# The first layer's score chunks in one group per pair: the next pair's first chunk is made a round ahead, in other banks

## What is computed

```python
q = einsum('qdh,bcd->bhcq', Q, x) * sq      # 16 heads of 64
k = einsum('qdh,bcd->bhcq', K, x) * sq
v = einsum('vdh,bcd->bhcv', V, x) * sv
att = where(causal, einsum('bhcq,bhCq->bhcC', q, k) / d_query, -inf)
y = einsum('bhcC,bhCv->bhcv', softmax(att), v)
z = einsum('dvh,bhcv->bcd', W, y) * scale   # back to 128 columns
```

## Time and profile before

| | |
|---|---|
| time, median of 3 runs | 1213.09 us (1210.03 to 1213.88) |
| profiled execution, first to last instruction | 1209.2 us |
| TensorE busy (matmul) | 1189.8 us, 98%, 8908 matmuls |
| TensorE loading weights (beside the matmuls) | 887.1 us, 73% |
| VectorE busy | 990.7 us, 82% |
| ScalarE busy | 819.7 us, 68% |
| GpSimd busy | 409.9 us, 34% |
| chain that ended last | TensorE 82%, VectorE 10%, ScalarE 4%, rest 4% |
| granted TensorE clock | full in all 40 slices |

### The profile page before, as it was taken

One profiled execution on the slowest core, in us unless ns is written; L12 is line 12 of the kernel. 1 busy time (PEld: TensorE's weight loads), 2 busy tenths in 40 slices (PEclk: granted clock), 3 DMA queues, 4 the chain that ended last, 5 costly groups with the idle time before them and its releaser, 6 DMA issues.

```text
span 1209.2 us, 23949 instructions
## 1 busy us (share of the span) xinstructions
PE 1189.8 (98%) x8908; PEld 887.1 (73%) x8908; DVE 990.7 (82%) x1918; ACT 819.7 (68%) x2174; POOL 409.9 (34%) x364
## 2 busy tenths in 40 slices
PE   8999999999999999999999999999999999999998
PEld 6777677767776777677767776777677767767766
DVE  6888588968886889688968896888788878988886
ACT  6785577567756775677567756775677768767875
POOL 2216420640064006400640064006400658535820
PEclk9999999999999999999999999999999999999999
DMA  7004300410041004200420042004200420000000
GB/s 258 1 30 134 97 1 21 132 61 2 20 134 62 1 19 134 62 1 19 135 62 1 20 134 62 1 17 136 62 1 16 138 62 2 7 12 19 1 11 27
DMA packets 44292, 63.93 MB, mean 53 GB/s; under 512 B 8144, under 2 KB 18384, under 8 KB 43920
## 3 DMA queue, kind: packets, MB, share of 16 engines
q1 hardware_dynamic: 44176, 62.39, 16.6%
HBM read 59.48 MB, written 2.88 MB: 52 GB/s over the span
## 4 chain that ended last, share of the span: by engine, by line
PE 82%; DVE 10%; ACT 4%; issue 2%; DMA 1%; SPq 1%; POOL 0%; DVEq 0%; ACTq 0%; POOLq 0%
PE psum L1435 14%; PE psum L1483 14%; PE psum L1505 12%; PE psum L64 9%; PE psum L66 9%; PE psum L65 9%; PE psum L1542 5%; DVE mneg L1123 2%; ACT probs L754 2%; PE psum L1444 2%; PE psum L1718 1%; DVE sg L1173 1%; PE psum L1509 1%; PE psum L1781 1%; DVE sg L1163 1%
## 5 line engine op out<-in xcount | busy, mean ns | idle before, releaser
L754 ACT ACTIVATE probs<-psum,mneg 128x512 f32<-128x512 f32 (+3 forms) x640 | 329.7, 529 | 127.1 <-DVE mneg L1123 122.5
L1123 DVE TENSOR_REDUCE mneg<-psum 128x2 f32<-128x1024 f32 (+2 forms) x320 | 253.6, 820 | 99.9 <-PE psum L1444 99.5
L1114 DVE COPY pt<-psum 128x512 f32<-128x512 f32 x320 | 205.2, 682 | 29.7 <-PE psum L1483 27.9
L1483 PE MATMUL psum<-ident,probs 128*128 128x128 f32 x1600 | 223.3, 278 | 6.1 <-DVE pt L1114 2.1
L1483 PEld LDWEIGHTS psum<-ident,probs 128*128 128x128 f32 x1600 | 176.5, 140 | 37.9 <-issue 19.5
L561 POOL TENSOR_TENSOR qk_lo<-sg,qk_hi 128x512 fp32r<-128x512 f32 x64 | 92.7, 1455 | 162.0 <-ACT qk_hi L798 162.0
L525 POOL TENSOR_TENSOR rstd<-var,mhalf 128x4 f32<-128x4 f32 x7 | 7.1, 1012 | 399.8 <-DVE var L1009 399.8
L1505 PE MATMUL psum<-pt,v_all 128*64 128x384 f32 (+5 forms) x1088 | 142.6, 412 | 0.0
L754 ACT ACTIVATION_READ_ACCUMULATOR probs<-psum,mneg 128x1 f32 x640 | 131.8, 206 | 0.0
L1435 PE MATMUL psum<-qk_hi 64*128 64x512 f32 (+7 forms) x640 | 121.6, 375 | 2.2 <-ACT probs L754 1.9
L1505 PEld LDWEIGHTS psum<-pt,v_all 128*64 128x64 f32 (+1 forms) x1088 | 69.5, 135 | 66.2 <-issue 50.7
(11 more groups left out here) (275 smaller groups left out, 2422.4 us busy)
## 6 DMA issues: line engine op xcount, KB each, us to landing
crow<-weights SPq DMA_DIRECT2D x256, 128.0 KB, 3.0
rrow<-sums SPq DMA_DIRECT2D x128, 128.0 KB, 3.0
gu_raw<-in_gu SPq DMA_DIRECT2D x1, 2176.0 KB, 11.5
x_all<-in_x SPq DMA_DIRECT2D x8, 256.0 KB, 6.4
out_rows<-x_all SPq DMA_DIRECT2D x7, 256.0 KB, 2.3
down_raw<-in_down SPq DMA_DIRECT2D x1, 1088.0 KB, 13.7
wqkv_raw<-in_wqkv SPq DMA_DIRECT2D x1, 896.0 KB, 6.8
wqkv_raw<-in_wqkv SPq DMA_DIRECT2D x1, 512.0 KB, 5.0
```

Of the source, the lines that this page charges most:

```text
L754: last = act.activation(probs[:, h * HALF + PROB[t]:h * HALF + PROB[t] + w], bank[score_bank(rnd, c) + h][:, o:o + w], ACT.Exp, bias=mneg[ ...
L1114: dve.tensor_copy(turned_rows(rnd)[:, s % 2, :, 3 - s // 2, :], turn_bank(rnd, s).rearrange("p (j q) -> p j q", q=P)).then_inc(pt_ready, 1)
L1123: last = dve.tensor_reduce(mneg_h[:, :, t], psum[:, b:b + 2, o:o + P * (t + 1)], AX, ALU.max, negate=True)
L1483: last = nc.tensor.transpose(turn_bank(rnd, s)[:, i * P:(i + 1) * P], probs[:, v:v + P], ident[:, :])
```

## The change

- The three chunks of a round become one group on TensorE (score_group): chunks 1 and 2 of pair n and chunk 0 of pair n+1. Each chunk's masks follow its own products. Chunk 0 uses banks 0 and 1, chunk 1 banks 2 and 3, chunk 2 banks 4 and 5.
- A round on TensorE is now: group; weighing of pair n-1; T0 and T1 of pair n; q and k of pair n+2; T4, T3 and T2 of pair n. Turns go to banks 7, 2, 6, 5, 4 for T0 to T4 (in round 0 to 6, 2, 7, 5, 4). Round 6 has the turn of the routing weights in place of q and k, round 7 that of the preceding batch's rows, both in bank 3; round 7's group has two chunks, and T4, T3 and T2 of its pair stand in units as before.
- q waits for the copy of y of pair n-1 (in round 0 for that of the accumulator), k for the copy of T0, chunk 1 for the copy of T1 (in round 7 for the copied routing weights too), chunk 2 for the copies of T4 and T3 and for the rests of pair n+1.
- ScalarE: exps of chunk 1, of chunk 2, copy_y(n-1), head 0 of the next pair's chunk 0 (next_exps), round_q(n+2), head 1 of that chunk, round_k(n+2), take_tile1(n).
- VectorE: maxima of chunks 1, 2 and the next pair's 0, routing step, copies of T0 and T1, inversion of sums, rest_q(n+2), copy of T3, rest_k(n+2), copy of T2.
- In units(b) T0, T1 and their waits are gone from the start, project_unit(b, 1) comes after a wait for the copy of T1 and for x1_ready in place of the waits for exponentials. The second layer keeps its banks and orders.

```diff
-SCORE_BANK = [0, 2, 0]
+SCORE_BANK = [0, 2, 4]
+SCORE_BANK1 = [0, 2, 0]
...
+        TURN_BANK0 = [7, 2, 6, 5, 4]
+        TURN_BANK0_FIRST = [6, 2, 7, 5, 4]
+
         def turn_bank(n, s):
+            if n < ROUNDS0:
+                return bank[(TURN_BANK0 if n % PAIRS else TURN_BANK0_FIRST)[s]]
...
-            return bank[6] if b < B - 1 else bank[7]
+            return bank[3] if b < B - 1 else bank[7]
+
+        WEIGHTS_BANK = bank[3]
...
-            if n < ROUNDS0 and n % PAIRS < 2:
-                return (bank[4], bank[5]) if n % PAIRS == 0 else (bank[6], bank[5])
+            if n < ROUNDS0 and n % PAIRS < 3:
+                return [(bank[4], bank[5]), (bank[6], bank[5]), (bank[7], bank[6])][n % PAIRS]
             return bank[6], bank[7]
...
+            def next_exps(rnd, h):
+
+                act.wait_ge(max_ready, max_count(rnd, 0))
+                act.wait_ge(turned, turn_count(rnd - 1, h))
...
                     if p == 0:
                         exps(n, 0)
+                        round_q(n + 1, SCALE0)
+                        round_k(n + 1)
+                    exps(n, 1)
+                    exps(n, 2)
+                    if p:
+                        copy_y(n - 1)
+                    elif b:
+                        copy_acc(b - 1)
                     if p < PAIRS - 1:
-                        round_q(n + 1, SCALE0)
-                    if p:
-                        take_tile1(n - 1)
-                        exps(n, 0)
+                        next_exps(n + 1, 0)
+                    if p < PAIRS - 2:
+                        round_q(n + 2, SCALE0)
                     if p < PAIRS - 1:
-                        round_k(n + 1)
-                    else:
+                        next_exps(n + 1, 1)
+                    if p < PAIRS - 2:
+                        round_k(n + 2)
+                    if p == PAIRS - 2:
                         copy_combt(b)
...
+                    take_tile1(n)
...
                     if p == 0:
                         row_maxima(n, 0)
-                        row_maxima(n, 1)
                         rest_q(n + 1, SCALE0)
                         rest_k(n + 1)
...
+                    row_maxima(n, 1)
+                    row_maxima(n, 2)
+                    if p < PAIRS - 1:
+                        row_maxima(n + 1, 0)
                     route(b, p)
+                    take_turned(n, [0, 1])
+                    invert_sums(n)
+                    if p < PAIRS - 2:
+                        rest_q(n + 2, SCALE0)
+                    if p < PAIRS - 1:
+                        take_turned(n, [3])
+                    elif b:
+                        add_rows(b - 1)
+                    if p < PAIRS - 2:
+                        rest_k(n + 2)
+                    if p < PAIRS - 1:
+                        take_turned(n, [2])
...
+            def turn_step0(n, s):
+
+                p = n % PAIRS
+                pe.wait_ge(exp_done, exp_count(n, [0, 1, 2, 2, 2][s]))
+                if s == 2:
+                    if p == 0:
+                        pe.wait_ge(qk_lo_ready, (n + 2) * 2 + 1)
+                    elif p < PAIRS - 2:
+                        pe.wait_ge(qk_lo_ready, (n + 2) * 2 + 1)
+                    else:
+                        pe.wait_ge(y_ready, n)
+                turn_blocks(n, s)
+
+            def score_group(n):
+
+                b, p = n // PAIRS, n % PAIRS
+                if p:
+                    pe.wait_ge(pt_ready, (n - 1) * (TURNS - 1) + 2)
+                if p == PAIRS - 1:
+                    pe.wait_ge(combt_ready, b + 1)
+                score0(n, 1)
+                if p:
+                    pe.wait_ge(pt4_ready, n)
+                    pe.wait_ge(pt_ready, (n - 1) * (TURNS - 1) + 3)
+                if p < PAIRS - 1:
+                    pe.wait_ge(qk_lo_ready, (n + 1) * 2 + 2)
+                score0(n, 2)
+                if p < PAIRS - 1:
+                    pe.wait_ge(exp_done, exp_count(n, 0))
+                    score0(n + 1, 0)
+
+            def slot(n):
...
                 if p == 0:
+                    first_head(b)
+                score_group(n)
+                if p:
+                    weigh_pair(n - 1)
+                elif b:
+                    project_out(b - 1, 3).then_inc(acc_done, 1)
+                turn_step0(n, 0)
+                turn_step0(n, 1)
+                if p < PAIRS - 2:
+                    if p:
+                        pe.wait_ge(y_ready, n)
+                    else:
+                        pe.wait_ge(acc_copied, b) if b else pe.wait_ge(logits_taken, 1)
+                    project_qk(n + 2, [0])
+                    pe.wait_ge(pt_ready, n * (TURNS - 1) + 1)
+                    project_qk(n + 2, [1])
+                elif p == PAIRS - 2:
+                    turn_weights(b)
+                elif b:
+                    turn_acc(b - 1)
                 if p < PAIRS - 1:
...
+                    turn_step0(n, 4)
+                    turn_step0(n, 3)
+                    turn_step0(n, 2)
...
             def first_head(b):
 
+                n = b * PAIRS
...
-                first_chunks(b)
-                score0(b * PAIRS, 1)
+                pe.wait_ge(qk_lo_ready, n * 2 + 2)
+                if b:
+                    pe.wait_ge(su_done, b * UNITS)
+                score0(n, 0)
+                pe.wait_ge(v_taken, (b + 1) * FILLS)
+                project_qk(n + 1, range(2))
                 if b:
                     project_out(b - 1, 2)
-                pe.wait_ge(v_taken, (b + 1) * FILLS)
-                project_qk(b * PAIRS + 1, range(2))
-                pe.wait_ge(exp_done, exp_count(b * PAIRS, 0))
-                score0(b * PAIRS, 2)
-                if b:
-                    project_out(b - 1, 3).then_inc(acc_done, 1)
```

More of the change, by code:

```diff
@@ L376, in max_count @@
         def max_count(n, c):
+            if n < ROUNDS0:
+                return n * NCH + c + 1
             return n * NCH + ([1, 2, 3] if first_round(n) else [1, 3, 2])[c]
         def score_bank(n, c):
-            return [6, 0, 6][c] if n >= ROUNDS0 and first_round(n) else SCORE_BANK[c]
+            if n < ROUNDS0:
+                return SCORE_BANK[c]
+            return [6, 0, 6][c] if first_round(n) else SCORE_BANK1[c]
         exp_count = max_count
@@ L756, in exps @@
                 last.then_inc(exp_done, 1)
+            def next_exps(rnd, h):
+                act.wait_ge(max_ready, max_count(rnd, 0))
+                act.wait_ge(turned, turn_count(rnd - 1, h))
+                t = CHUNKS[0][0]
+                o, s = h * HALF + PROB[t], slice(h * TILES + t, h * TILES + t + 1)
+                last = act.activation(probs[:, o:o + T], bank[score_bank(rnd, 0) + h], ACT.Exp, bias=mneg[:, s], accum_out=rsum[:, rnd % 2, s])
+                if h:
+                    last.then_inc(exp_done, 1)
             def take_values(b, fills):
@@ L811, in copy_combt @@
                 act.wait_ge(combt_done, b + 1)
-                act.activation(combt, bank[7][:, 0:P], ACT.Copy).then_inc(combt_ready, 1)
+                act.activation(combt, WEIGHTS_BANK[:, 0:P], ACT.Copy).then_inc(combt_ready, 1)
             def first_layer(b):
@@ L1523, in project_unit @@
                     pe.wait_ge(su_done, n - 1)
-                else:
-                    pe.wait_ge(exp_done, exp_count((b + 1) * PAIRS - 1, 2 - u))
                 half_unit(b, u, 0)
@@ L1585, in turn_weights @@
                 pe.wait_ge(comb_ready, b + 1)
-                nc.tensor.transpose(bank[7][:, 0:P], rexp[:, :, :].rearrange("p t e -> p (t e)"), ident[:, :]).then_inc(combt_done, 1)
+                nc.tensor.transpose(WEIGHTS_BANK[:, 0:P], rexp[:, :, :].rearrange("p t e -> p (t e)"), ident[:, :]).then_inc(combt_done, 1)
             def score0(n, c):
                 score_chunk(n, c, n % 2, ROWS0)
-            def first_chunks(b):
-                n = b * PAIRS
-                pe.wait_ge(qk_lo_ready, n * 2 + 2)
-                if b:
-                    pe.wait_ge(su_done, b * UNITS)
-                score0(n, 0)
-            def slot(n, head):
+            def turn_step0(n, s):
[26 more added lines that the diff above has]
+            def slot(n):
                 p = n % PAIRS
```

71 lines of the change are left out of this document (9 added, 62 removed).

## The result

| | before | after |
|---|---|---|
| median of 4 runs each | 1212.49 us (1210.03 to 1213.88) | 1233.1 us (1230.07 to 1233.91) |
| ratio, 95% interval | | 1.0165 (1.0146 to 1.0183) |
| profiled execution, first to last instruction | 1209.2 us | 1228.2 us |
| TensorE / VectorE / ScalarE busy | 1189.8 / 990.7 / 819.7 us | 1196.0 / 984.5 / 807.2 us |
| weighing to weighing, rounds 2 to 5 of a batch | 8.76 us | 9.05 to 9.08 us |

A forecast was written before the change was run, and what follows sets the result against it. TensorE set the pace before; the change closes a circle of 9.08 us a round through TensorE, VectorE and ScalarE. Seven batches at +2.5 (17.7) and the first at +1.2 make 1213.1 + 18.9 = 1232.0 us, range 1226 to 1239.

The forecast's parts named there:

- The circle: Rounds 2 to 5: q through TensorE, VectorE, ScalarE's copy of y to the next q takes 9.08 us, against 8.76 before.
- The head of a batch: Start of each batch: q of pair 2 starts 10.25 us after the first score product, 8.51 before, so +1.74.
- TensorE alone would be there at 9.8: Start of a batch: by its own work alone TensorE would reach q of pair 2 at 9.8 us.
- The tail: From q of pair 2 to the batch's end: +1.60 for five turns, -1.31 for less work, +0.5 at last chunk 1.
- The sum: Whole kernel: +2.5 us a batch, 17.7 for seven, +1.2 for the first, together +18.9.
- half a loss: First batch, with no accumulator to wait for and rounds already lengthened by weight copies: +1.2 us.
- Net 0.22 a round: without waits a round would take 8.54: TensorE's own work in a round: 0.26 us removed, 0.04 added, giving 8.54 without waits.
- the exit: Rounds 1 to 7: one exit from score products is removed as the first chunk no longer stands alone, 0.10 us.
- the new passage: Inside the score group, from masks to products between the two old chunks: adds 0.04 us, taken between 0 and 0.10.
- the second rival: Rounds: from q to q takes 8.54 us or less, nothing closes, 12 us are won: 1201 us, chance 0.09.
- The rest of q ends just before T2 needs its bank: Each round's last turns: VectorE's rest of q is done in time for T2, which needs that bank.
- the 0.5 us that TensorE was to stand: Rounds 2 to 5: TensorE idles about 0.5 us before q's first product, released by ScalarE's copy of y.

The follow-up runs named there:

- the kernel with the rests late: Changed kernel with q in bank 3, weights and accumulator copied earlier, chunk 2 not waiting for the next pair's rests in rounds 1 to 6: 1203.8 us.
- the first change of ScalarE's order: Changed kernel with the copy of y (in round 0 of the accumulator) ahead of chunk 2's exponentials: 1231.98 us, 1.0163 of before.
- the one with two copies moved and rests late in its second run: Changed kernel with q in bank 3, weights and accumulator copied earlier, wait for the rests behind chunk 2, timed again: 1204.01 us, 0.9938 of before.
- the one with q first in round 0: Kernel with q in bank 3, both copies and the rests' wait moved, plus q of pair 2 rounded before chunk 0 in round 0: 1201.76 us.

## Why the prediction was right

**The circle.** Predicted 9.08, measured 9.06, and each leg by its own size. TensorE from q to VectorE's copy of T3: 2.56 (408.13 to 410.69), predicted 2.54 and 0.04. VectorE to the maxima: 1.81 (to 412.50), predicted 1.79. Maxima to ScalarE: 1.31 (to 413.81), as predicted. ScalarE to q: 3.38 (to 417.19), predicted 3.34 and 0.06. What the profile of before shows in pieces could be put together in another order because the durations didn't change. The two kernels with y and tile 1 doubled show that it is the place of the copy, the one with an instruction more before T2 that VectorE's leg is on it, and q's own bank that the circle closes through the shared one.

**The head of a batch.** q of pair 2 starts 10.23 us after the first score product (388.84 to 399.07), predicted 10.25, and waits for the accumulator:

```profile
388.84 0.50 PE L1457 MATMUL psum<-qk_hi 64*128 64x512 f32 x2
...
394.49 0.39 PE L1457 MATMUL psum<-qk_hi 64*128 64x256 f32 x2 [0.17 <-DVE qk_lo L1131]
...
399.07 0.50 PE L65 MATMUL psum<-xt_hi,wqkv_hi 128*128 128x512 f32 x1 [0.24 <-ACT rrow L824]
```

Chunk 2's wait for k of pair 1 (394.49) is there and stays hidden, as said. With the accumulator copied early, q comes at 9.81 (381.08 to 390.89 in the kernel with the rests late); "TensorE alone would be there at 9.8".

**The tail.** From the last q to the last pair's chunk 1 10.65 us (444.38 to 455.03), predicted 10.60; the wait is worth 0.41 by experiment, predicted 0.5.

**The sum.** The last weighing of the last batch comes 19.15 us later than before, 1.10 of it in the first batch and 18.05 in the seven others; predicted 18.9, of it 1.2 and 17.7. The rest of the kernel takes as long as before (269.2 for 269.3). The first batch's 1.2 was a guess ("half a loss"), and that it fits is luck: its first weighing comes 2.29 later (32.49 for 30.20), the next five distances are together 0.16 shorter, the last two 1.02 shorter.

**What was off.** Two steps, which partly hide each other. The step "Net 0.22 a round: without waits a round would take 8.54" was too small: it is 8.49, net 0.27. The mis-sized term is the masks: they took 0.17 and 0.27 in a round before (419.21 to 419.38, 422.86 to 423.13 in the earlier trace rows), together 0.44; by the prediction they would take 0.10 less for the exit and 0.04 more for the new passage, 0.38; in the rows of the kernel with the rests late they take 0.10, 0.06 and 0.17, together 0.33. So the passage priced at 0.04 adds nothing. The forecast did not hang on it, since the circle is longer than either. The rule of the Trainium skill (TensorEngine Tiling, Key Properties: changing the tiling mode drains the engine) stood for the second rival; the trace agrees with it, by 0.27 us a round for one entry and one exit less, once the circle is open; the draining itself no row shows. And the step "The rest of q ends just before T2 needs its bank" was wrong: the rest ends at 410.45 (409.76 + 0.69 on VectorE), T2's four turns start at 410.60 and not at 410.49, where eight turns of 0.109 would have brought them, and the twelve turns take 1.54 (409.62 to 411.16) where they take 1.40 in the kernel that gives q its bank (409.92 to 411.32). In the changed kernel this 0.14 is off the circle, as VectorE takes T2 only at 411.90. It decided the first change of ScalarE's order, where the same wait closed the next circle. Of the 0.5 us that TensorE was to stand, 0.40 lies before q, 0.14 here.

**The expectations.** Those of the circle as it stands were right within 0.02 us a round. Those of what comes next when it is opened were 0.1 to 0.4 a round too good, each for the same reason: they counted the circle that was opened and not the next longest.

## What to carry to other kernels

Before a bank is shared between a late reader and an early writer, follow the circle once, from the writer's start through every engine back to it, with the durations of the old trace in the new order, and compare its length with the busiest engine's own work: the idle shares of the other engines (VectorE 20%, ScalarE 34% here) say nothing of it. An edit that opens a circle is worth only the distance to the next longest, which is to be added up beforehand; here a buffer of its own opened every circle through that buffer, and each change of order only one. A wait is to stand directly ahead of what needs it: moved behind one chunk, it gave 0.11 us a round, 0.4% of the whole.

## What the runs showed that was not expected

**The clock at the start.** Of the thirteen profiles with the grouped order seven have a stretch at half clock, 1.2 for 2.4 GHz, between 23 and 32 us from the start; six of the thirteen and the kept profile of the kernel before have none. Two kernels of the same rounds over that time, the one with two copies moved and rests late in its second run, and the one with q first in round 0 (stretch, us, TensorE's busy us, granted clock, DMA share, GB/s):

```profile
20.00:24.00 4.00, 2.88 (x28) 1.00 1.15 279
24.00:28.00 4.00, 3.23 (x23) 0.61 0.47 118
```

```profile
20.00:24.00 4.00, 2.12 (x29) 1.00 1.15 286
24.00:28.00 4.00, 2.97 (x28) 1.00 0.45 109
```

TensorE had more to do before the clock fell in the first (2.88 of 4 us) than in the second (2.12), where it did not fall. The grouped order waits there for 1.9 us in one piece for the rest of k of pair 1, where the kernel before waits 1.1 at most; whether that wait is the cause stays open, for all thirteen have it. Nor is the kernel before free of lower clocks: of its 19 executions beside the first experiments six have a mean granted clock of 1.000 and spans of 1208.2 to 1209.2 us, the other thirteen 0.996 to 0.999 and 1209.4 to 1212.7; where it fell in these is not on record. The last weighing of the first batch comes at 90.60 in the first and 89.23 in the second, of which 0.35 at most is the edit's: some 1 us of the difference between these two profiles may be the clock's. In the kernel with one more instruction before T2, which also has the stretch, the first weighing comes at 34.95 instead of 32.49 in the changed kernel, and its span is 26.7 longer where 40 rounds of 0.61 give 24.4.

**The units' part of a batch varies.** With the rounds equal to 0.02 us, a batch of the changed kernel took 123.2 to 123.9 us. The difference lies in the experts' units: from the last weighing of a batch to the next batch's first score product it takes 47.35 to 48.00 us in batches 2 to 7, from there to the first weighing always 15.71 to 15.73. That is as large as many edits are worth. A single execution tells a round's length well and a kernel's time badly.
